# Layer 0 of a two-layer graph network: VectorE multiplies all eight pairs of gathered chunks by their attention weights, ScalarE none

## The chip, the cores and the metric

The program runs on one core of one Trainium2 chip. The core has a matrix engine (TensorE, PE in the profile), three engines for elementwise work (VectorE = DVE, ScalarE = ACT, GpSimd = POOL), a queue for plain transfers (SP) and 16 DMA engines. The metric is the time of one whole execution on the device, in microseconds (us), as the median of several runs. Lower is better.

## What is computed

There are 6250 nodes with 512 features each and 100000 edges. Two layers run one after the other; the change is in the first, a graph attention layer with 8 heads of 64 columns. Cut to what matters:

```python
for h in range(8):
    feat = x @ W[h]
    logit = leaky_relu((feat @ a1)[src] + (feat @ a2)[dst], 0.2)
    m = segment_max(logit, src)
    e = exp(logit - m[src])
    att = e / segment_sum(e, src)[src]
    agg = segment_sum(att[:, None] * feat[dst], src)
    outs.append(relu(agg))
x = x + concatenate(outs, axis=1)
```

The second layer (a graph convolution and a linear attention over the first 256 nodes, with two batch norms) is the same before and after, as is the sorting of the edges that goes ahead of the first.

## The kernel before

**Data.** The edges are sorted by source node and laid out in chunks of 128 slots. Sixteen chunks are a batch, and there are 55 batches. Two chunks of one tile of 128 source nodes are a pair, or "lot"; a batch has eight lots, numbered 0 to 7. For each chunk GpSimd issues one gather (line 503) of 128 rows of 528 floats from `feat_table` in HBM into the ring `ring`, a part of the buffer `big` with room for two batches. A row holds 8 heads of 65 columns (64 features and a one, so that the weights are summed along) and 8 logits of the target node.

**One pass.** The function `pass_batch` of each engine handles two batches at once: it sums up the lots of the batch `this` and prepares the weights of the batch `nxt`. The order on each engine is written out by hand, lot by lot (`a` = 0 to 7). The lot `a` of `this` needs three steps:

- its 2 x 520 columns in the ring are multiplied by their attention weights, in place. On VectorE this is `weigh(b, a)` (line 678), one instruction for both chunks with the weights read from PSUM. It is done for lots 0 to 5 (`OWN` = 6). For lots 6 and 7 it is ScalarE's `weigh_late` (line 553), 16 instructions for a lot, one for each chunk and head, since ScalarE takes one scale for each partition and so one column of weights at a time. ScalarE reads them from `late_weights` in SBUF, into which VectorE copies them once a batch (line 676) ahead of `weigh(b, 0)`;
- TensorE's `lot(b, a)` (line 796): four float32 matmuls against the one-hot matrix of the slots' nodes, into `psA` for even and `psB` for odd lots;
- VectorE's `add_lot(b, a)` (line 688): the sums in PSUM are added to the tile's rows in `acc`. `lot(b, a + 2)` may begin only then, and GpSimd may issue the two gathers of the next batch but one into the same place of the ring as soon as the matmuls of the lot are through (`lot_ps`).

**The weights of the next batch** are made in between, in a chain that goes from engine to engine: ScalarE copies the gathered logits (564), TensorE turns them (765, behind lot 3), ScalarE copies the result (566), VectorE takes running maxima over it (`local_runs`, 616 to 621), TensorE sums the chunks' ends over partitions (769), VectorE carries the maxima over (`carry_runs`, 628 to 640), TensorE spreads them (774), VectorE takes the running maxima again (`find_tops`, 647 to 658), ScalarE makes the exponential (545), and TensorE turns the weights into PSUM (779). Only then can `weigh(nxt, 0)` start. TensorE also turns the one-hot matrix (756) and looks up logits (747) for the batch after, for which VectorE makes the transposed one-hot matrix (600) in two halves.

On VectorE the order from lot 3 on is: `add_lot(this, 3)`, `local_runs`, `carry_runs`, `add_lot(this, 4)`, second half of line 600, `find_tops`, `add_lot(this, 5)`, `add_lot(this, 6)`, line 676, `weigh(nxt, 0)`, `weigh(nxt, 1)`, `add_lot(this, 7)`. On ScalarE the 16 scalings of lot 6 stand at the start of a pass, and those of lot 7 behind the copies of the indices (527).

Of the kernel before, what the change touches and what calls it, by code (L numbers as in the profile page):

```python
# [92 lines left out]
def build(nc, x, src, dst, W0, att_w, norm1_g, norm1_b, norm2_g, norm2_b, W_conv, b_conv, Wq, Wk, Wv, Wo, proj, out):  # L93
    with ExitStack() as ctx:
        def sb(name, shape, dt):
            return ctx.enter_context(nc.sbuf_tensor(name, shape, dt))
# [4 lines left out]
        def sem(name):  # L101
            return ctx.enter_context(nc.semaphore(name))
# [143 lines left out]
        late_weights = sb("late_weights", [P, 4 * H], F32)  # L246
# [101 lines left out]
        late_known = sem("late_known")  # L348
        late_weighted = sem("late_weighted")
# [8 lines left out]
        OWN = LB - 2  # L358
# [166 lines left out]
        def layer0_scalar(act, link, links, clear_rest):  # L525
# [21 lines left out]
            def weigh_late(b, a):  # L547
                act.wait_ge(late_known, b(1, 1))
                for u in (2 * a, 2 * a + 1):
                    for h in range(H):  # L550
                        part = ring[:, b.k, u, h * HO:(h + 1) * HO]
                        at = (u - 2 * OWN) * H + h
                        ins = s.activation(part, part, ACT.Copy, scale=late_weights[:, at:at + 1])  # L553
                    ins.then_inc(late_weighted, 1)

            def feed(b, this=None):

                if this:
                    for a in range(OWN, LB - 1):
                        weigh_late(this, a)  # L560
# [9 lines left out]
                if this:  # L570
                    weigh_late(this, LB - 1)
# [18 lines left out]
            for a in range(OWN, LB):  # L590
                weigh_late(batch(BATCHES - 1), a)

            layer1_scalar(act, link, links, put_indices)

        def layer0_vector(dve, link, links):
# [75 lines left out]
            def weigh(b, a):  # L671
                if a == 0:
                    dve.wait_ge(weights_turned, b(1, 1))
                    dve.wait_ge(scale_done, b(1, 1))
                    wait_count(dve, late_weighted, b(2 * (LB - OWN), 0))
                    v.tensor_copy(late_weights[:, 0:2 * (LB - OWN) * H], weight_ps[b.k][:, 2 * OWN * H:P]).then_inc(late_known, 1)
# [14 lines left out]
            def pass_batch(this, nxt):  # L691
# [4 lines left out]
                for a in range(LB):  # L696
                    if this:
                        if 2 <= a + 2 < OWN:
                            weigh(this, a + 2)
                        if a == 0:  # L700
                            rescale(this, tiles[0])
# [38 lines left out]
        def layer0_tensor(pe, turn_fields):  # L740
# [44 lines left out]
            def lot(b, a):  # L785
# [3 lines left out]
                if a < OWN:  # L789
                    pe.wait_ge(weighted, b(OWN, a + 1))  # L790
                else:
                    pe.wait_ge(late_weighted, b(2 * (LB - OWN), 2 * (a + 1 - OWN)))
# [1729 lines left out]
```

## Time and profile before

| | us |
|---|---|
| median of 3 runs | 3545.59 |
| lowest and highest of them | 3543.25, 3546.13 |
| span of the profiled execution | 3572.6 |

| engine, whole span | busy us | share |
|---|---|---|
| PE matmul | 2678.2 | 75% |
| PE weight load | 1671.6 | 47% |
| DVE | 2439.1 | 68% |
| ACT | 994.4 | 28% |
| POOL | 1863.4 | 52% |

The span is that of one execution under the profiler, 27 us over the median of the runs, which are timed without it; the time around its span is not recorded separately. The batches of layer 0 fill the stretch from 472 to 1904 us. In the rows below a line of the timeline gives the start, the duration, the engine, the line of the code and the tiles, and in brackets how long the engine sat idle before it and what ended that. "Remote" stands where no event in the profile was found that ended the wait, "issue" where the engine waited for nothing that the profile shows.

### The profile page before, as it was taken

What the parts mean: (1) busy time and instruction counts of PE and PEld (TensorE: products, weight loads), DVE (VectorE), ACT (ScalarE), POOL (GpSimd) and SP (SyncE); (2) the same over time, 40 slices, a digit from 0 to 9 for tenths busy, and PEclk for the clock granted to TensorE, in tenths of its full rate; (3) what the DMA queues carried; (4) which work ended last, traced back from release to release, by engine and by line L of the source; (5) the groups of instructions that cost most, each with busy time, mean ns of one, the idle gap of its engine ahead of it and who ended that gap; (6) DMA issues with size and microseconds to landing.
All of it is one profiled execution on the core that took longest, in us unless ns stands there. A gap on an engine that the chain in (4) does not pass through costs nothing. (4 is left out here: it accounts for less than half of the span.)

```text
span 3572.6 us, 49438 instructions
## 1 busy us (share of the span) xinstructions
PE 2678.2 (75%) x11236; PEld 1671.6 (47%) x11237; DVE 2439.1 (68%) x4270; ACT 994.4 (28%) x3078; POOL 1863.4 (52%) x1887
## 2 busy tenths in 40 slices
PE   6887367777787777778777777777777778778991
PEld 4554246665665666566666642322233333233440
DVE  9999956766666666667678745555555556566668
ACT  6733334443444444434443420000000000000220
POOL 0000255555555555555556446666666666663667
PEclk8988678998899898989898888888888889989995
DMA  5110366666666666666655856555555655654226
GB/s 183 46 40 31 103 175 188 189 184 187 175 187 186 183 190 180 187 183 186 184 189 189 265 161 183 171 174 174 173 171 174 175 170 175 177 169 152 68 68 246
DMA packets 243499, 588.70 MB, mean 165 GB/s; under 512 B 57744, under 2 KB 82832, under 8 KB 243400
## 3 DMA queue, kind: packets, MB, share of 16 engines
q0 software_dynamic: 133120, 443.52, 42.8%
q1 hardware_dynamic: 110280, 144.14, 12.3%
q14 instruction: 72, 0.59, 0.1%
q8 instruction: 27, 0.44, 0.1%
HBM read 533.43 MB, written 54.10 MB: 164 GB/s over the span
## 5 line engine op out<-in xcount | busy, mean ns | idle before, releaser
L503 POOL DMA_INDIRECT big<-feat_table,idx x880 | 835.6, 950 | 1031.9 <-ACT idx L527 409.1
L1131 POOL DMA_INDIRECT big<-h_table,idx x784 | 741.6, 946 | 473.5 <-issue 229.3
L796 PE MATMUL psA<-big,onehot 128*128 128x260 f32 x1760 | 481.3, 421 | 92.4 <-DVE big L678 72.9
L796 PE MATMUL psB<-big,onehot 128*128 128x260 f32 x1760 | 496.2, 431 | 28.4 <-DVE acc L688 22.6
L553 ACT ACTIVATE big<-big,late_weights 128x65 f32<-128x65 f32 x1760 | 434.1, 341 | 0.0
L796 PEld LDWEIGHTS psA<-big,onehot 128*128 128x128 f32 x1760 | 352.5, 207 | 171.8 <-issue 91.0
L796 PEld LDWEIGHTS psB<-big,onehot 128*128 128x128 f32 x1760 | 358.9, 214 | 102.2 <-DVE acc L688 34.9
L1854 PE MATMUL psA<-big,onehot 128*128 x556 | 316.9, 694 | 111.2 <-issue 83.9
L1854 PE MATMUL psB<-big,onehot 128*128 x556 | 299.6, 662 | 82.1 <-issue 42.9
L527 ACT CAST idx<-minorB 128x8 int32 (+1 forms) x101 | 20.3, 203 | 1154.6 <-DMA big<-h_table,idx 1154.6
L1566 DVE TENSOR_TENSOR acc<-acc,psA 128x512 f32 x278 | 190.6, 686 | 154.3 <-issue 64.1
L1566 DVE TENSOR_TENSOR acc<-acc,psB 128x512 f32 x278 | 190.6, 685 | 129.6 <-issue 42.1
L1854 PEld LDWEIGHTS psA<-big,onehot 128*128 128x128 f32 x556 | 112.5, 216 | 267.2 <-issue 266.0
L1854 PE MATMUL psCD<-big,onehot 128*128 x276 | 161.3, 669 | 85.8 <-issue 57.6
L1854 PEld LDWEIGHTS psB<-big,onehot 128*128 128x128 f32 x556 | 111.6, 212 | 232.9 <-issue 232.8
L678 DVE TENSOR_TENSOR big<-big,psCD 128x1040 f32<-128x1040 f32 x168 | 203.8, 1227 | 2.1 <-issue 2.0
L688 DVE TENSOR_TENSOR acc<-acc,psB 128x520 f32 x220 | 152.0, 691 | 69.5 <-PE psA L796 34.6
L678 DVE TENSOR_TENSOR big<-big,psE 128x1040 f32<-128x1040 f32 x162 | 196.6, 1227 | 0.0
L2436 PE MATMUL psB<-big 128*128 128x512 f32 x392 | 186.1, 619 | 0.0
L1882 PE MATMUL psA<-big 128*128 128x512 f32 x392 | 180.3, 603 | 0.3 <-ACT big L1297 0.3
L688 DVE TENSOR_TENSOR acc<-acc,psA 128x520 f32 x220 | 152.5, 693 | 37.4 <-issue 6.8
L1854 PE MATMUL psE<-big,onehot 128*128 x276 | 157.5, 655 | 13.0 <-issue 6.9
(442 smaller groups left out, 3805.5 us busy)
## 6 DMA issues: line engine op xcount, KB each, us to landing
nodes_all<-slot_nodes SPq DMA_DIRECT2D x56, 512.0 KB
big<-feat_table,idx POOLq DMA_INDIRECT x880
feat_table<-big SPq DMA_DIRECT2D x49, 264.0 KB, 2.1
x_table<-acc SPq DMA_DIRECT2D x49, 256.0 KB, 3.7
h_table<-big SPq DMA_DIRECT2D x49, 256.0 KB, 3.9
big<-h_table,idx POOLq DMA_INDIRECT x784
big<-h_table SPq DMA_DIRECT2D x49, 256.0 KB, 2.6
big<-x_table SPq DMA_DIRECT2D x49, 256.0 KB, 4.4
```

Of the source, the lines that this page charges most:

```text
L503: g.indirect_dma_start(ring[:, b.k, q * SB + u, :], None, feat_table, bass.IndirectOffsetOnAxis(ap=idx[:, 2 * b.k + q, u:u + 1], axis=0)). ...
L527: s.copy(idx[:, q, :], minor_t[:, :, bass.ds(r, 1)].rearrange("p b a -> p (b a)")).then_inc(signal, 1)
L553: ins = s.activation(part, part, ACT.Copy, scale=late_weights[:, at:at + 1])
L678: v.tensor_tensor(pair, pair, weight_ps[b.k][:, 2 * a * H:(2 * a + 2) * H] .rearrange("p (b h) -> p b h", h=H).unsqueeze(3).broadcast_to([ ...
L688: v.tensor_tensor(d, d, (psA, psB)[a % 2][:, :].rearrange("p (u w) -> p u w", u=2)[:, :, 0:HALF_W], ALU.add).then_inc(lot_added, 1)
L796: ins = pet.matmul(psum[:, 512 * hf:512 * hf + HALF_W], onehot[:, q, u % SB, :], ring[:, b.k, u, HALF_W * hf:HALF_W * (hf + 1)], start=(u ...
L1131: g.indirect_dma_start(big[:, place:place + D], None, h1_table, bass.IndirectOffsetOnAxis(ap=idx[:, r.c % CHUNK_CYCLE, b:b + 1], axis=0)). ...
L1566: v.tensor_tensor(d, d, lot1_sums(r, b), ALU.add).then_inc(lot1_added, 1)
L1854: pet.matmul(lot1_sums(r, b), onehot[:, r.q, b, :], big[:, bass.ds(at[b % 4], D)], start=True, stop=True).then_inc(lot1_ps, 1)
L1882: ins = pet.matmul(psA[:, q * 512:(q + 1) * 512], aggT[:, q, k * P:(k + 1) * P], Wc_s[:, k, :], start=(k == 0), stop=(k == KD - 1))
L2436: pet.matmul(psB[:, q * D:(q + 1) * D], hTbuf[:, q, k * P:(k + 1) * P], W4[:, k, :, :].rearrange("p h o -> p (h o)"), start=(k == 0), stop ...
```

## The change

VectorE runs `weigh` for lots 6 and 7 too, so that each batch has eight of them and `OWN` goes. The 32 scalings of a batch on ScalarE, the copy of 32 columns of weights into `late_weights` and that tile itself, and two semaphores go as well. TensorE waits for `weighted` ahead of each lot.

```diff
@@ ScalarE
-            def weigh_late(b, a):
-                act.wait_ge(late_known, b(1, 1))
-                for u in (2 * a, 2 * a + 1):
-                    for h in range(H):
-                        part = ring[:, b.k, u, h * HO:(h + 1) * HO]
-                        at = (u - 2 * OWN) * H + h
-                        ins = s.activation(part, part, ACT.Copy, scale=late_weights[:, at:at + 1])
-                    ins.then_inc(late_weighted, 1)
-
             def feed(b, this=None):
-                if this:
-                    for a in range(OWN, LB - 1):
-                        weigh_late(this, a)
                 act.wait_ge(rows_arrived[b.k], b.pair(16 * CH, 16 * CH))
...
                     put_indices(minorA, b(2, 4 + q), 2 * b.k + q, idx2)
-                if this:
-                    weigh_late(this, LB - 1)
                 make_weights(b)
@@ VectorE
                     dve.wait_ge(scale_done, b(1, 1))
-                    wait_count(dve, late_weighted, b(2 * (LB - OWN), 0))
-                    v.tensor_copy(late_weights[:, 0:2 * (LB - OWN) * H], weight_ps[b.k][:, 2 * OWN * H:P]).then_inc(late_known, 1)
...
                 for a in range(LB):
                     if this:
-                        if 2 <= a + 2 < OWN:
+                        if a + 2 < LB:
                             weigh(this, a + 2)
@@ TensorE, lot
-                if a < OWN:
-                    pe.wait_ge(weighted, b(OWN, a + 1))
-                else:
-                    pe.wait_ge(late_weighted, b(2 * (LB - OWN), 2 * (a + 1 - OWN)))
+                pe.wait_ge(weighted, b(LB, a + 1))
```

VectorE's queue between `add_lot(this, 3)` (the last 128x520 row at the top) and the end of `local_runs`, in the pass of an odd batch. Before:

```order
L688 TENSOR_TENSOR acc<-acc,psB 128x520
L130 ISA
L130 TENSOR_LOAD tables
L615 REGISTER_ALU
L616 SCALAR_TENSOR_TENSOR alphas<-alphas 128x128 [waits logit_kept]
```

With the change (line 665 is the former 688, 655 the former 678, 595 the former 616):

```order
L665 TENSOR_TENSOR acc<-acc,psB 128x520
L130 ISA
L130 TENSOR_LOAD tables
L655 TENSOR_TENSOR big<-big,psCD 128x2x520
L594 REGISTER_ALU
L595 SCALAR_TENSOR_TENSOR alphas<-alphas 128x128 [waits logit_kept]
```

The multiplication for lot 6 stands ahead of the wait for `logit_kept`. Further down in the same pass, VectorE from the end of `carry_runs` (640) to `find_tops` (647). Before:

```order
L640 TENSOR_TENSOR look_space<-look_space 8x16 [waits carry_step]
L684 REGISTER_ALU
L687 REGISTER_ALU [waits lot_added]
L688 ISA [waits lot_ps]
L688 TENSOR_TENSOR acc<-acc,psA 128x520
L385 REGISTER_ALU
L600 TENSOR_SCALAR big<-nodes_all,iota_col 128x1024 [waits turned_ps]
L647 TENSOR_TENSOR look_space<-psE,chunk_of 128x32 [waits carry_done]
```

With the change (619 is the former 640, 579 the former 600, 626 the former 647):

```order
L619 TENSOR_TENSOR look_space<-look_space 8x16 [waits carry_step]
L661 REGISTER_ALU
L664 REGISTER_ALU [waits lot_added]
L665 ISA [waits lot_ps]
L665 TENSOR_TENSOR acc<-acc,psA 128x520
L655 TENSOR_TENSOR big<-big,psCD 128x2x520
L381 REGISTER_ALU
L579 TENSOR_SCALAR big<-nodes_all,iota_col 128x1024 [waits turned_ps]
L626 TENSOR_TENSOR look_space<-psE,chunk_of 128x32 [waits carry_done]
```

The multiplication for lot 7 stands between `add_lot(this, 4)` and the wait for `turned_ps`.

## Rows read from the trace of the kernel before

**Rows 1.** Page, costliest groups: count, then busy us and mean ns of one.

```profile
L503 POOL DMA_INDIRECT big<-feat_table,idx x880 | 835.6, 950 | 1031.9 <-ACT idx L527 409.1
...
L553 ACT ACTIVATE big<-big,late_weights 128x65 f32<-128x65 f32 x1760 | 434.1, 341 | 0.0
...
L678 DVE TENSOR_TENSOR big<-big,psCD 128x1040 f32<-128x1040 f32 x168 | 203.8, 1227 | 2.1 <-issue 2.0
...
L678 DVE TENSOR_TENSOR big<-big,psE 128x1040 f32<-128x1040 f32 x162 | 196.6, 1227 | 0.0
```

**Rows 2.** Line 676, even batches: min/median/max ns, first and last start.

```profile
L676 DVE COPY late_weights<-psCD x28: 181/190/192, 472.2 to 1887.2; 128x32 f32<-128x32 f32 x28
```

**Rows 3.** Windows, length; busy us (instructions) of PE, PEld, DVE, ACT, POOL; PEclk, DMA, GB/s.

```profile
472.18:1867.29 1395.11, 1084.52 (x5721) 850.32 (x5721) 951.77 (x1908) 597.00 (x2173) 800.61 (x845) 0.90 0.64 185
1867.29:1887.24 19.95, 18.16 (x110) 14.21 (x109) 17.70 (x38) 11.26 (x41) 3.11 (x4) 1.00 0.21 67
```

**Rows 4.** Waits, 460 to 1910 us: total us, times, longest us.

```profile
POOL big L503 <- PE psA L796: 148.7, 87, 13.8
POOL big L503 <- PE psB L796: 128.5, 71, 3.0
...
POOL big L503 <- remote: 109.4, 45, 3.0
...
DVE big L600 <- remote: 97.6, 30, 9.9
...
DVE look_space L630 <- remote: 79.3, 27, 4.6
DVE late_weights L676 <- remote: 73.4, 27, 3.8
...
DVE alphas L616 <- issue: 25.0, 11, 3.8
```

**Rows 5.** Timeline, a batch whose long stop is ahead of line 600.

```profile
1790.17 0.18 DVE L676 COPY late_weights<-psCD 128x32 f32<-128x32 f32 x1
...
1805.67 0.23 PE L769 MATMUL psE<-look_space,head_of 128*8 128x32 f32 x2 [0.98 <-DVE look_space L621]
1805.83 0.62 PE L756 MATMUL psCD<-ident_bf,big 128*128 128x128 bf16 x8
...
1807.57 0.16 DVE L630 TENSOR_TENSOR look_space<-psE,look_space 8x16 f32<-8x16 f32 x1 [1.89 <-remote]
...
1808.35 0.70 DVE L688 TENSOR_TENSOR acc<-acc,psA 128x520 f32 x1
...
1809.14 0.95 POOL L503 DMA_INDIRECT big<-feat_table,idx  x1 [0.30 <-issue]
...
1811.99 0.49 DVE L600 TENSOR_SCALAR big<-nodes_all,iota_col 128x1024 bf16<-128x1024 bf16 x1 [2.94 <-remote]
...
1812.86 0.94 POOL L503 DMA_INDIRECT big<-feat_table,idx  x1 [2.77 <-PE psA L796]
...
1816.31 0.18 DVE L676 COPY late_weights<-psE 128x32 f32<-128x32 f32 x1
```

**Rows 6.** Timeline, a batch whose long stops are ahead of lines 630 and 676.

```profile
1422.04 0.19 DVE L676 COPY late_weights<-psCD 128x32 f32<-128x32 f32 x1 [1.62 <-remote]
...
1439.22 0.16 DVE L630 TENSOR_TENSOR look_space<-psE,look_space 8x16 f32<-8x16 f32 x1 [2.81 <-remote]
...
1443.71 0.33 PE L779 MATMUL psE<-ident_wide,look_space 128*128 128x128 f32 x1
...
1448.84 0.19 DVE L676 COPY late_weights<-psE 128x32 f32<-128x32 f32 x1 [3.78 <-remote]
```

**Rows 7.** Timeline, line 630 in the batch without gathers.

```profile
1880.62 0.16 DVE L630 TENSOR_TENSOR look_space<-psCD,look_space 8x16 f32<-8x16 f32 x1 [0.27 <-PE psCD L769]
```

**Rows 8.** Timeline: the shortest of the batches under gathers, its two ends.

```profile
1027.59 0.19 DVE L676 COPY late_weights<-psE 128x32 f32<-128x32 f32 x1 [1.63 <-remote]
...
1051.84 0.18 DVE L676 COPY late_weights<-psCD 128x32 f32<-128x32 f32 x1
```

More of the change, by code:

```diff
@@ L245, in build @@
         factor = carve("look", 1)
-        late_weights = sb("late_weights", [P, 4 * H], F32)
         factors = carve("look", H)
@@ L347, in build @@
         weighted = sem("weighted")
-        late_known = sem("late_known")
-        late_weighted = sem("late_weighted")
         lot_ps = sem("lot_ps")
@@ L357, in build @@
         RING_CREDIT = 2 * LB
-        OWN = LB - 2
         FREE_CHUNKS = SB * D // ROW_W
@@ L589, in layer0_scalar @@
                     feed(Batch(i, c + 1), Batch(i, c))
-            for a in range(OWN, LB):
-                weigh_late(batch(BATCHES - 1), a)
             layer1_scalar(act, link, links, put_indices)
```

## The prediction

> **What bounds the kernel now.** I read the costliest groups first, then the windows over layer 0, then the waits there, then the timeline of single batches. Only layer 0's batches are touched: line 676 runs once in each of the 55 batches, first at 472.2 and last at 1887.2 us [rows 2], so 54 batches take (1887.2 - 472.2) / 54 = 26.2 us each.
>
> No engine is full there. Up to 1867 us, in 1395 us, VectorE is busy 952, which is 17.8 us of each 26.2 us batch (68%), TensorE 1085, ScalarE 597, GpSimd 801 [rows 3]. So VectorE has some 8 us of idle time in a batch, and the question is whether the added work falls into it. The batch that runs while nothing is gathered any more takes 19.95 us, with VectorE busy 17.70 of them [rows 3]: without gathers the hand-made order runs almost without a stop on VectorE, and the other 6.2 us of a normal batch come with the gathers.
>
> GpSimd issues 16 gathers a batch, each 0.95 us [rows 1] with 0.30 us behind it (the idle time shown in front of one in the middle of a run [rows 5]): 16 x 1.25 = 20.0 us. The rest is stops, in which it waits for a lot to be through so that its place in the ring is free: 148.7 + 128.5 + 109.4 = 387 us in all, 7.2 a batch [rows 4].
>
> The timeline shows that GpSimd's long stop and VectorE's end together. In one batch TensorE ran the transposes of line 756 at 1805.83 for 0.62 us, but VectorE, which waits for them alone ahead of line 600, went on only at 1811.99; GpSimd issued its last allowed gather at 1809.14 and the next at 1812.86 [rows 5]. The lot that it waited for stands right behind the transposes on TensorE. In another batch VectorE stops ahead of 630 until 1439.22 and ahead of 676 until 1448.84, though TensorE had run line 779 at 1443.71 [rows 6]. Without gathers the stop ahead of 630 is 0.27 us [rows 7]. So what TensorE finishes late in a long run of gathers is heard of by the others only when that run has ended. I call this **the hold**. The rows show it, not its cause. It costs VectorE 97.6 us ahead of 600, 79.3 ahead of 630 and 73.4 ahead of 676 [rows 4].
>
> By the Trainium skill (TensorE: Matmul & The Clock Gate, section "The cost: per-tile semaphore tail") increments on completion of matmuls follow each other by some 26 ns, so that a signal of TensorE would be heard at once. This trace does not agree if the records of TensorE are taken as they stand: the gap from 1806.45, where the transposes end, to 1811.99 is 5.5 us. If the page is right here as well, the stops have another cause, and the second rival below is what would follow.
>
> **The change part by part.**
>
> *Two more multiplications on VectorE:* 2 x 1.227 us [rows 1] = 2.45 us a batch, 135 us for all 55. VectorE's busy time in a batch goes from 17.8 to 20.1 us of 26.2.
>
> *The copy of the weights goes:* 0.19 us on VectorE [rows 2], on the path, since weigh(nxt, 0) stands behind it. Part of it overlaps the next instruction, so 0.1 to 0.19; I take 0.15. TensorE also loses one or two register instructions a lot, which I cost at nothing: it is idle in every batch; if they were on the path this would be a gain of some 0.1 us a lot at most.
>
> *ScalarE's scalings go:* 434.1 us of busy time [rows 1], 7.9 a batch. They lie beside other work: those of lot 6 are followed by a wait for the gathered rows, those of lot 7 by one for VectorE's maxima, and no row of the waits has line 553 as the releaser. I take 0. The bounds are 0 and a gain of the same 0.15 us a batch, if one of ScalarE's copies comes earlier now. TensorE's lots 6 and 7 now wait for VectorE, but both products are ready before the add that the lot waits for as well, so the cost is 0; without that cover it would be 1.23 us.
>
> *Place one, weigh 6 ahead of local_runs.* Where VectorE waits there anyway (25.0 us, 11 times, 2.3 each), the 1.23 us are hidden. Elsewhere line 616 and with it TensorE's 769 come 1.23 us later. Behind that stands everything in the chain: 630 to 640, 774, find_tops, add 5, lot 7.
>
> *Place two, weigh 7 ahead of line 600.* It delays line 600 and find_tops by 1.23 us, unless VectorE would have waited there.
>
> Batches come in two kinds. In **27 of them** VectorE stops ahead of 676, 2.7 us on average, and 630 has a long stop as often, 2.9 us on average [rows 4]. The example took 1448.84 - 1422.04 = 26.80 us, with stops of 2.81 and 3.78 us [rows 6]. If the hold ends when the gathers say so, both additions vanish here: 1.23 before the first stop, 1.23 before the second. What stays is the copy: 27 x -0.15 = -4 us.
>
> In **the other 27** of the 54 there is no stop ahead of 676, and the long one is ahead of 600 (30 times, 3.3 us [rows 4]). The example took 1816.31 - 1790.17 = 26.14 us [rows 5]. Here place one matters. TensorE's 769 stood at 1805.67 and its signal came at 1807.57, already late; that of 756, issued 0.16 us behind, came at 1811.99. Moved by 1.23 us, 769 would stand at 1806.90, later than 756 did, so I expect its signal at 1811.9 too. Then VectorE does after the hold what it did in it: line 630 to the end of add 4, 1807.57 to 1809.05 [rows 5], 1.48 us, and weigh 7, 1.23 us, so that line 600 comes 2.7 us later. That is the upper end for this kind: 27 x 2.7 = 73 us. The lower end is that such a batch then becomes one of the first kind, where later stops give most of it back: 26.80 - 26.14 = 0.66 us, 27 x 0.66 = 18 us. No row is nearer to one of these, so I take the middle, 46 us.
>
> Sum: 46 - 4 = **+42 us** (between +14 and +69), +0.8 us a batch. The last batch prepares nothing, and its two added multiplications pair with adds at 1.23 + 0.69 us a lot, about the 1.9 that a lot takes on TensorE: 0 to 2 us, I take 2. So +44. Against the profiled execution: 3572.6 + 44 = 3617 us of span. The runs without the profiler are 27 us shorter (median 3545.6), and I expect the same distance after: **3590 us**, 1.2% slower.
>
> **The rivals.**
>
> *Fully hidden (no change).* If 769 still slips through ahead of the hold in the second kind, both additions fall into stops there too: place one into 630's, place two into 600's. It leaves 54 x -0.15 = -8 to 0 us: 3538 to 3546. For it: VectorE's stops ahead of 616, 630, 600 and 676 sum to 275 us, twice what is added. Against it: 769 would have to move by 1.23 us in a stretch where 0.16 us already made 4.4 us of difference.
>
> *Fully added.* If the stops begin where VectorE arrives and keep their length, instead of ending at a set time, nothing is hidden: 54 x (2.45 - 0.15) = 124 us, 3670 us. For it: the whole chain goes through VectorE, and in the batch without gathers it was idle only 2.25 us [rows 3]. Against it: GpSimd's stop ends together with VectorE's.
>
> *Faster.* The mechanism is the number of GpSimd's stops. Later sums on VectorE shift when lots become free; where two stops of the gathers merge into one, a batch is like the shortest that the trace has, 1051.84 - 1027.59 = 24.25 us [rows 8], 1.95 less than the mean. The price is -1.95 us a batch; against the forecast's 44 us it decides from 23 of the 54 batches. In a third more of them without the cost, 18 x 1.95 = 35: 3510 us. For it: the period is set by gathers and stops, not by VectorE's work. Against it: nothing in the change brings a lot forward; it can only be luck of phase.
>
> *That it doesn't do what it says* can be left out: the order shows eight multiplications a batch on VectorE and none on ScalarE.
>
> **How the numbers follow.** The forecast (partly hidden, 3560 to 3615) has a chance of 0.55, fully added or worse 0.15, fully hidden 0.15, faster by merged stops 0.15. The range leaves out the lower two thirds of the last and what is beyond full addition: 3530 to 3670. A measurement of this kernel can tell 0.2%, 7 us, from no change. Faster by more than that: 0.15 and a little of the hidden case, 0.17; within: 0.13; slower: 0.70.
>
> **What would show it right or wrong in the profile of the changed kernel.** Multiplications on VectorE 440 at 1.23 us, ScalarE's busy time down by 434 us; if one of them lasts longer than 1.23, a term is missing. Period of the batches near 27.0 us; 26.1 would speak for fully hidden, 28.5 for fully added. The stops ahead of 600 should shrink and those ahead of 630 and 676 become more frequent (over 35 of 54 each): place one pushed 769 into the hold. If instead the four stops on VectorE keep their total of 275 us, the additions were not absorbed anywhere. The batch without gathers should take 19.95 + 2.3 = 22.3 us, since little is idle there. The forecast is wrong at its root if GpSimd's stops (7.2 us a batch) shrink while VectorE's work grows.

## The result, and the profile after

| | before | after |
|---|---|---|
| median of 20 runs each, us | 3542.82 | 3551.26 |
| lowest and highest | 3531.82, 3558.64 | 3537.79, 3563.67 |
| ratio, 95% interval | | 1.0025 [1.0015, 1.0034] |
| span of the profiled execution | 3572.6 | 3551.2 |
| mean batch in that execution, us | 26.3 | 26.2 |

The change costs 8 us, a fifth of the 44 forecast. The time is inside the range given and the sign is right, but what happened is the rival "fully hidden", not the forecast. (That the profiled execution after is the shorter one is the scatter of single executions: on one chip a second pair of profiled executions gave 3538.0 before and 3551.7 after.) A batch is measured here from the start of one `weigh(nxt, 0)`, the first multiplication of VectorE for a batch, to the start of the next. There are 54 such stretches; the mean is over the first 53, and the last one, in which almost nothing is gathered, is given by itself further down.

The page of the kernel after, the engines' busy time and the costliest groups; lines 499 and 655 are the former 503 and 678, as in [rows 1]:

```profile
PE 2649.2 (75%) x11236; PEld 1651.3 (46%) x11237; DVE 2559.8 (72%) x4325; ACT 571.9 (16%) x1318; POOL 1863.9 (52%) x1887
...
L499 POOL DMA_INDIRECT big<-feat_table,idx x880 | 836.9, 951 | 1019.5 <-ACT idx L523 407.8
...
L655 DVE TENSOR_TENSOR big<-big,psCD 128x1040 f32<-128x1040 f32 x224 | 273.1, 1230 | 37.5 <-remote 33.8
L655 DVE TENSOR_TENSOR big<-big,psE 128x1040 f32<-128x1040 f32 x216 | 263.3, 1229 | 42.6 <-remote 42.6
```

There are 224 + 216 = 440 multiplications, at 1.23 us as before. ScalarE's busy time is down from 994.4 to 571.9, VectorE's up from 2439.1 to 2559.8. So the work moved as said and at the duration said; the open question is only where 121 us of VectorE's time went.

Windows over layer 0 in the kernel after, columns as in [rows 3]:

```profile
472.00:1904.00 1432.00, 1099.58 (x5916) 865.57 (x5916) 1108.60 (x2030) 194.94 (x486) 808.94 (x852) 0.91 0.63 184
```

DMA share and GB/s are within 0.01 and 1 of [rows 3]. VectorE is now busy 77% of the stretch. Its waits and GpSimd's, 460 to 1910 us, to be held against [rows 4]; line 609 is the former 630, 579 the former 600, 626 the former 647:

```profile
POOL big L499 <- PE psB L770: 175.9, 84, 3.4
...
POOL big L499 <- PE psA L770: 119.2, 107, 12.9
...
POOL big L499 <- remote: 79.9, 34, 2.6
...
DVE big L655 <- remote: 76.4, 34, 2.4
...
DVE look_space L609 <- remote: 40.3, 18, 3.5
...
DVE look_space L626 <- remote: 35.9, 8, 5.4
...
DVE big L579 <- remote: 19.7, 13, 13.2
```

GpSimd's stops are where they were: 375 us in these three rows against 387. VectorE's have shrunk: ahead of line 579 from 97.6 to 19.7, ahead of 609 from 79.3 to 40.3. (Of the 97.6 and the 19.7 one stop each, 9.9 and 13.2 us, lies ahead of the first of these batches; within them it is 87.7 against 6.5.) All idle gaps of VectorE over 0.3 us between the first and the last batch, added up from the timeline, went from 401 to 274 us, by 127. That is about what was added (121). **The added work went into VectorE's stops, and the stops of the gathers, which set the period, stayed.**

The timeline of one batch of the kernel after, columns as in [rows 5], between the two first multiplications:

```profile
1026.93 0.94 POOL L499 DMA_INDIRECT big<-feat_table,idx  x1 [1.10 <-PE psA L770]
...
1035.67 0.95 POOL L499 DMA_INDIRECT big<-feat_table,idx  x1 [0.30 <-issue]
...
1037.10 0.28 PE L746 MATMUL psCD<-look_space,head_of 128*8 128x32 f32 x2 [2.57 <-DVE look_space L600]
1037.31 1.03 PE L733 MATMUL psCD<-ident_bf,big 128*128 128x128 bf16 x8
...
1038.41 0.16 DVE L609 TENSOR_TENSOR look_space<-psCD,look_space 8x16 f32<-8x16 f32 x1 [1.31 <-PE psCD L746]
...
1039.15 0.94 POOL L499 DMA_INDIRECT big<-feat_table,idx  x1 [2.53 <-remote]
...
1039.89 1.23 DVE L655 TENSOR_TENSOR big<-big,psE 128x1040 f32<-128x1040 f32 x1
1041.04 0.55 DVE L579 TENSOR_SCALAR big<-nodes_all,iota_col 128x1024 bf16<-128x1024 bf16 x1
...
1044.16 0.33 PE L756 MATMUL psCD<-ident_wide,look_space 128*128 128x128 f32 x1
...
1047.83 2.39 DVE L655 TENSOR_TENSOR big<-big,psCD 128x1040 f32<-128x1040 f32 x2 [2.34 <-remote]
```

Line 746 is the former 769, 733 the former 756, 756 the former 779. The ends' matmul (746, it sums the chunks' ends) is over at 1037.38 and line 609 goes on at 1038.41, 1.03 us later. Weigh 7 runs at 1039.89, and behind it line 579, which used to stand still for the transposes [rows 5], starts with no wait at all: by then their signal has come. The stop that is left is the one ahead of the next batch's first product, 2.34 us.

### The profile page after: what moved, and what is told of

It reads as the page before. It is cut to its first block and busy times, and to the rows that moved or that the text cites. A ratio compares the mean times of both kernels' runs of the same rounds, so it can differ in the third digit from the quotient of the medians.

```text
span 3551.2 us, 47733 instructions
## 1 busy us (share of the span) xinstructions
PE 2649.2 (75%) x11236; PEld 1651.3 (46%) x11237; DVE 2559.8 (72%) x4325; ACT 571.9 (16%) x1318; POOL 1863.9 (52%) x1887
## 5 line engine op out<-in xcount | busy, mean ns | idle before, releaser
L770 PE MATMUL psA<-big,onehot 128*128 128x260 f32 x1760 | 453.2, 402 | 98.5 <-DVE big L655 80.1
L770 PE MATMUL psB<-big,onehot 128*128 128x260 f32 x1760 | 506.0, 438 | 11.1 <-issue 6.4
L770 PEld LDWEIGHTS psA<-big,onehot 128*128 128x128 f32 x1760 | 331.4, 196 | 174.4 <-DVE big L655 95.0
L770 PEld LDWEIGHTS psB<-big,onehot 128*128 128x128 f32 x1760 | 368.8, 220 | 82.3 <-issue 19.5
L1828 PE MATMUL psA<-big,onehot 128*128 x556 | 306.2, 675 | 101.0 <-issue 63.8
L655 DVE TENSOR_TENSOR big<-big,psCD 128x1040 f32<-128x1040 f32 x224 | 273.1, 1230 | 37.5 <-remote 33.8
L655 DVE TENSOR_TENSOR big<-big,psE 128x1040 f32<-128x1040 f32 x216 | 263.3, 1229 | 42.6 <-remote 42.6
L1828 PEld LDWEIGHTS psA<-big,onehot 128*128 128x128 f32 x556 | 110.9, 213 | 254.1 <-issue 253.8
L1828 PEld LDWEIGHTS psB<-big,onehot 128*128 128x128 f32 x556 | 109.6, 208 | 237.3 <-issue 236.7
L1540 DVE TENSOR_TENSOR acc<-acc,psCD 128x512 f32 x138 | 94.6, 685 | 72.2 <-issue 29.6
```

The source lines that it names most:

```text
L655: v.tensor_tensor(pair, pair, weight_ps[b.k][:, 2 * a * H:(2 * a + 2) * H] .rearrange("p (b h) -> p b h", h=H).unsqueeze(3).broadcast_to([ ...
L770: ins = pet.matmul(psum[:, 512 * hf:512 * hf + HALF_W], onehot[:, q, u % SB, :], ring[:, b.k, u, HALF_W * hf:HALF_W * (hf + 1)], start=(u ...
L1540: v.tensor_tensor(d, d, lot1_sums(r, b), ALU.add).then_inc(lot1_added, 1)
L1828: pet.matmul(lot1_sums(r, b), onehot[:, r.q, b, :], big[:, bass.ds(at[b % 4], D)], start=True, stop=True).then_inc(lot1_ps, 1)
```

## The experiments

Each of the five groups of runs had a chip of its own, and these are of **two kinds**; all runs of a group are of the same kind. On kind A the kernel before takes 3538 to 3544 us, as in the result above; on kind B it takes 3032 to 3038. Ratios are to the kernel before on the same chip. The runs do not say what makes a chip one or the other. The recorded expectations speak of three theories: A, the stops that come with the gathers hide VectorE's added work; B, ScalarE's relief gives as much back as the added work costs, gathers or not; C, added after the first group, on a chip without late signals GpSimd's 16 issues set the batch.

| kernel | kind | median us | ratio [95%] | batch us |
|---|---|---|---|---|
| ng_before | B | 2978.57 | 0.9812 [0.9785, 0.9838] | 19.53 |
| ng_after | B | 3064.20 | 1.0083 [1.0052, 1.0114] | 21.14 |
| minus2 | B | 3031.95 | 0.9991 [0.9980, 1.0002] | 20.57 |
| plus2 | B | 3182.68 | 1.0487 [1.0457, 1.0517] | 23.30 |
| before_again | A | 3549.31 | 1.0011 [0.9995, 1.0027] | 26.08 |
| after_again | A | 3553.78 | 1.0015 [0.9992, 1.0037] | 26.09 |
| plus1 | A | 3552.37 | 1.0014 [0.9993, 1.0034] | 26.12 |
| sprows_after | A | 3278.47 | 0.9242 [0.9195, 0.9290] | 21.35 |
| after_third | B | 3068.63 | 1.0127 [1.0100, 1.0153] | 21.19 |
| plus2_again | B | 3183.16 | 1.0499 [1.0479, 1.0518] | 23.29 |
| plus4 | B | 3294.39 | 1.0866 [1.0847, 1.0885] | 25.29 |
| paced_after | B | 3062.54 | 1.0104 [1.0085, 1.0123] | 21.05 |
| eight_after | A | 3397.91 | 0.9609 [0.9579, 0.9639] | 23.33 |
| spaced_after | A | 3828.10 | 1.0825 [1.0796, 1.0854] | 31.24 |
| plus2_c | A | 3572.98 | 1.0117 [1.0086, 1.0149] | 26.54 |
| plus4_c | A | 3626.54 | 1.0257 [1.0225, 1.0290] | 27.34 |
| pace4_before | B | 3196.05 | 1.0522 [1.0505, 1.0540] | 23.46 |
| pace2_before | B | 3353.63 | 1.1045 [1.1026, 1.1063] | 26.46 |

The theory from here on: on the chip of the result the gathers and the late signals set the end of VectorE's stops, so that work put ahead of them is free until the stops are used up. The rival: VectorE's chain sets the period, and something else hid the work.

### First group (kind B): no gathers, and VectorE's work per batch changed by two products

Both kernels without gathers leave out those of the batches 2 to 54, so that old rows are summed; in ScalarE's code the wait for them goes to a constant:

```diff
-            with pool.Fori(1, BATCHES // 2) as i:
-                for c in range(2):
-                    gather_batch(Batch(i, c))
-            gather_batch(batch(BATCHES - 1))
...
-                act.wait_ge(rows_arrived[b.k], b.pair(16 * CH, 16 * CH))
+                act.wait_ge(rows_arrived[b.k], 16 * CH)
```

> Kernel before, but GpSimd gathers rows only for batches 0 and 1; the later batches weigh and sum what lies in the ring already, so their neighbours' features are left out. Theory A (the stops that come with the gathers hide VectorE's added work): every batch runs as the last one of the kernel before did, 19.95 us instead of 26.2, so about 54 x 6.25 = 337 us less than 3543, near 3205 us. Theory B (the added work costs nothing because the freed ScalarE gives as much back elsewhere, gathers or not): the same for this kernel.

> The changed kernel with gathers for batches 0 and 1 only, as the other one without gathers. Theory A: with the gathers' stops gone the added 2.3 us a batch are bare, so 124 us over the kernel before without gathers, near 3330 us (up to 54 x 4 = 219 more if its last batch of 24.0 us is the measure). Theory B: within 20 us of the kernel before without gathers.

Windows 500 to 1450 us, columns as in [rows 3], of ng_before and then of ng_after:

```profile
500.00:1450.00 950.00, 885.08 (x5268) 692.43 (x5267) 860.92 (x1759) 542.89 (x1999) 0.00 (x0) 1.00 0.09 29
```

```profile
500.00:1450.00 950.00, 833.88 (x4857) 653.22 (x4856) 889.98 (x1664) 157.27 (x405) 0.00 (x0) 0.98 0.08 26
```

Without gathers VectorE is busy 91% of the time before and 94% after, and a batch grows by 21.14 - 19.53 = 1.61 us. So the added products do cost when nothing else bounds, though 1.6 and not the 2.3 that I took for the batch without gathers: before, VectorE still had idle time, 45 us in gaps over 0.3 us, of which 17 are left after.

The kernel minus2 is the kernel after without the products of lots 6 and 7 (nobody multiplies them):

```diff
-                        if a + 2 < LB:
+                        if a + 2 < LB - 2:
...
-                pe.wait_ge(weighted, b(LB, a + 1))
+                pe.wait_ge(weighted, b(LB - 2, min(a + 1, LB - 2)))
```

> The changed kernel, but lots 6 and 7 are not multiplied by their weights by any engine, which part of layer 0 is left out. Theory A: VectorE's 2.45 us a batch were hidden, so nothing comes back: 3535 to 3551 us. Theory B: the work is on the path and ScalarE's relief stays, so 124 us less: 3427 us.

The kernel plus2 (and plus1, plus4) is the kernel after with two (one, four) small multiplications ahead of each of the products of lots 6 and 7, into a tile that nobody needs then; four of them measured 2.1 us a batch, and plus1's two 0.9:

```diff
+                if a >= LB - 2:
+                    for n in range(2):
+                        wait_count(dve, spared, b(4, (a - LB + 2) * 2 + n))
+                        v.tensor_tensor(maxd[...390 columns...], iota_row[...], weight_ps[b.k][...],
+                                        ALU.mult).then_inc(spared, 1)
```

> The changed kernel with four more VectorE products of 390 columns a batch, two ahead of each of the multiplications of lots 6 and 7, written to a tile that nobody reads; some 0.66 us each with the wait, 2.6 us a batch, 143 us in all. Theory A: VectorE still has 276 us of stops in layer 0, 5.1 us a batch, but some of these are shorter than what is put ahead of them, so a part shows: 20 to 80 us over the changed kernel, 3570 to 3630 us. Theory B: all of it shows, 3690 us.

Window of minus2, same columns:

```profile
500.00:1450.00 950.00, 858.78 (x4998) 667.93 (x4996) 818.30 (x1618) 164.43 (x414) 703.48 (x739) 0.99 0.80 237
```

The kernel minus2 takes as long as the kernel before. On kind B, then, ScalarE's 32 scalings do not bound the kernel before, since a kernel without them and without the products in their place is no faster; GpSimd does, busy 703 of 950 us, which with 0.30 us behind each of the 739 gathers is 925. Its 16 x 1.25 = 20.0 us are all but 0.57 of the batch. The kernel after, at 21.2 us, is above that floor and bound by VectorE, and so plus2 costs in full: 3182.7 - 3068.6 (after_third, below) = 114 us for the 54 x 2.1 = 113 added.

### Second group (kind A): the two kernels again, one product's worth more, and plain transfers

> The kernel before, unchanged, to have its trace from the chip that this call gets. The runs without gathers were on a chip where it takes 3032 us instead of 3543. If the chip is like that one: theory C (no hold there, the batch is paced by GpSimd's 16 issues of 1.25 us) expects batches of 20.3 to 20.8 us and hardly any stop of GpSimd; if the hold is there too, batches of 26 us or more stops. Ratio to itself 1.00.

> The changed kernel, unchanged. Theory C on a chip without the hold: VectorE's chain is barely shorter than GpSimd's 20.3 us there, so the added work shows in part: the batch of 21.1 us of the changed kernel without gathers, against 20.6: 54 x 0.5 to 0.9 = 27 to 49 us, ratio 1.009 to 1.016. Theory A in its old form (always hidden): ratio 1.00. On a chip with the hold both expect 1.0025 again.

> The changed kernel with two more VectorE products of 390 columns a batch, one ahead of each multiplication of lots 6 and 7, 1.3 us a batch, written to a tile that nobody reads. Without the hold, theory C: VectorE is the longest already, all of it shows, 54 x 1.3 = 70 us over the changed kernel. With the hold: under 20 us over it, since VectorE has 5.1 us of stops a batch.

For sprows_after SP fetches rows of the table in plain transfers of the same bytes; GpSimd gathers nothing behind batch 0. Other rows are summed than the reference's:

```diff
+            def plain_rows(b, lots):
+                for a in lots:
+                    sp.wait_ge(lot_ps, b(LB, a + 1))
+                    for u in (2 * a, 2 * a + 1):
+                        sp.dma_start(ring[:, b.k, u, :], feat_table[u * P:(u + 1) * P, :]).then_inc(rows_plain[b.k], 16)
```

> The changed kernel with the gathers of batches 1 to 54 replaced by as many plain transfers of the same size from the SP queue (always the rows of the first 16 tiles, so the choice of rows by edge is left out). If GpSimd's indirect gathers with 1.25 us of issue each pace the batch: batches of 21.1 us as without gathers. If the bytes do it (4.3 MB a batch), the same batches as with gathers: 26 us on a chip with the hold, 20.6 to 21.3 on one without.

The three kernels from before_again to plus1 cannot be told apart, at 26.08, 26.09 and 26.12 us a batch. The kernel plus1 has 0.9 us more on VectorE in each than the kernel after, and its median is within 2 us of that kernel's (added in full it would be 51). With plain transfers a batch falls to 21.35 us, 4.7 less than with gathers. Its timeline, the ends' matmul and the line that waits for it, and its window:

```profile
1006.57 0.23 PE L756 MATMUL psCD<-look_space,head_of 128*8 128x32 f32 x2 [1.97 <-DVE look_space L610]
1006.83 0.16 DVE L619 TENSOR_TENSOR look_space<-psCD,look_space 8x16 f32<-8x16 f32 x1 [0.27 <-PE psCD L756]
```

```profile
1000.00:1300.00 300.00, 264.62 (x1521) 207.05 (x1521) 279.04 (x522) 50.36 (x126) 0.00 (x0) 0.97 0.73 229
```

The matmul ends at 1006.80 and is heard at 1006.83. The DMA engines move more than before (229 GB/s against 185) and still no signal is late. So it is neither the bytes nor the load of the DMA engines; it goes with the gathers that GpSimd issues.

### Third group (kind B): the kernel after again, more work, and increments between gathers

> The changed kernel, unchanged, for the trace and the ratio on this call's chip. With the hold (kernel before at 3543 us): ratio 1.00 to 1.003, batches of 26.1 to 26.3 us. Without it (kernel before at 3032 us): theory C says batches of 21.1 to 21.4 us against 20.5, ratio 1.009 to 1.016.

> The changed kernel with four more products of 390 columns a batch on VectorE, 2.6 us a batch. With the hold: its stops on VectorE are 5.1 us a batch, of which the half-sized addition used up 0.8 without any loss of time; theory A says a batch of 26.3 to 27.0 us, 0 to 38 us over the changed kernel. Without the hold: 150 us over the kernel before, as measured once.

> The changed kernel with eight such products a batch, 5.2 us. VectorE's own work is then 25.4 us a batch, near the 26.2 us of the batch. With the hold, theory A: the stops cannot hide all of it, 27.5 to 29 us a batch, 70 to 150 us over the changed kernel. If stops keep a fixed length instead of ending at a set time, all 5.2 us show, 280 us. Without the hold: 290 us over the kernel before.

```diff
+                            if not under_sort:
+                                for _ in range(5):
+                                    pool.sem_inc(hold, 1)
```

> The changed kernel with five semaphore increments ahead of each gather on GpSimd, so that gathers are issued some 1.5 us apart and no longer 1.25. If the hold comes from gathers issued faster than they are carried out (a backlog), it goes: batches of 24 to 25 us on a chip with it, 60 to 120 us less. If it comes from each gather whatever the distance, the batch gets longer by 16 x 0.25 = 4 us, 200 us more. Without the hold: GpSimd's issue becomes the bound, 24 us a batch, 180 us over the kernel before.

The same place in after_third, which has its gathers at 1.25 us like all others:

```profile
1019.96 0.23 PE L746 MATMUL psE<-look_space,head_of 128*8 128x32 f32 x2 [1.97 <-DVE look_space L600]
1020.23 0.16 DVE L609 TENSOR_TENSOR look_space<-psE,look_space 8x16 f32<-8x16 f32 x1 [0.27 <-PE psE L746]
```

0.04 us from end to start, and so in all of its batches: on kind B there is no hold. Against the kernel after, plus2 costs 114 us and plus4 226, for 113 and 54 x 4.1 = 221 us of added work. There VectorE's chain is the bound and nothing is hidden. The change itself costs 36 us there, a third of the 121 added, since the first part of it fills VectorE's idle time beside GpSimd's 20.0 us.

I had meant paced_after to spread the gathers on a chip with the hold. It shows nothing: it ran on one without, and the increments did not spread them. GpSimd's rows:

```profile
1000.71 1.02 POOL L502 DMA_INDIRECT big<-feat_table,idx  x1 [0.30 <-issue]
1002.03 0.97 POOL L502 DMA_INDIRECT big<-feat_table,idx  x1 [0.30 <-issue]
```

Its batch is 21.05 us, where 24 was expected of spread gathers on such a chip. On plus4 the expectation was 290 us over the kernel before; measured were 262.

### Fourth group (kind A): half the gathers, gathers further apart, and more work

```diff
+                            if not under_sort and q == 1:
+                                continue
```

leaves out the gathers of chunks 8 to 15 of each batch from batch 2 on (ScalarE then waits for half the rows), so that half the rows summed are old, and for spaced_after a small fill on GpSimd, with a wait for it, ahead of each gather:

```diff
+                                g.memset(maxd[...64 columns...], 0.0).then_inc(paced, 1)
+                                pool.wait_ge(paced, b(2 * SB, q * SB + u + 1 - 4 * SB))
+                                pool.sem_inc(hold, 1)
```

> The changed kernel with gathers for the first 8 of 16 chunks of each batch from batch 2 on; the other 8 keep old rows, so their neighbours are left out. With late signals (kernel before at 3543 us): if they need a long run of gathers, runs of at most 8 gathers leave time for them, batches near the 21.2 us that the chain needs by itself, some 270 us less than the changed kernel. If every gather delays signals, batches of 23 to 25 us, 70 to 170 us less. Without late signals (3032 us): 21.0 to 21.2 us a batch, 0 to 10 us less than the changed kernel.

> The changed kernel with a fill of 64 columns on GpSimd and a wait for it ahead of each gather, so that gathers stand some 1.5 us apart and no longer 1.25. With late signals: if they come from a backlog of gathers (265 KB each 1.25 us is some 216 GB/s), it goes, and a batch takes 16 x 1.5 = 24 to 25 us, 60 to 120 us less than the changed kernel. If each gather delays them whatever the distance, the batch gets longer by 16 x 0.25 = 4 us, 200 us more. Without late signals: GpSimd's 24 us are the bound, 3220 us.

> The changed kernel with 2.1 us more work on VectorE in a batch (four products of 390 columns). On the chip without late signals a batch took 23.3 us with it, so as long as that is under the 26.3 us of the late signals, theory A (the stops end at a time that the gathers set) expects 0 to 38 us over the changed kernel. If only stops of a fixed length hide work, all of it shows: 114 us over.

> The changed kernel with 4.1 us more on VectorE in a batch. On the chip without late signals a batch took 25.3 us with it. Theory A: still below 26.3, but few stops are left to hide it: 27 to 28 us a batch, 40 to 100 us over the changed kernel. Fixed stops: 225 us over.

In eight_after all eight gathers of a batch come in one run. Its first and its last, and the ends' matmul behind them:

```profile
1009.88 0.94 POOL L501 DMA_INDIRECT big<-feat_table,idx  x1 [12.63 <-PE psA L772]
...
1018.62 1.01 POOL L501 DMA_INDIRECT big<-feat_table,idx  x1 [0.30 <-issue]
...
1019.47 0.23 PE L748 MATMUL psCD<-look_space,head_of 128*8 128x32 f32 x2 [2.00 <-issue]
...
1021.30 0.16 DVE L611 TENSOR_TENSOR look_space<-psCD,look_space 8x16 f32<-8x16 f32 x1 [1.84 <-remote]
```

The last gather is issued by 1019.63, the matmul ends at 1019.70 and is heard at 1021.30, 11.4 us behind the start of the run. In the batch of the kernel after above it is the same: a run of eight from 1026.93, line 609 at 1038.41, 11.5 us later. In [rows 5] it is 11.6 us. Some signals are heard inside a run, as in [rows 5] that of 769; what is still held then is let go at a time that depends on the length of the run. In the traces of before, before_again, after, after_again and plus1 the first stop of VectorE or ScalarE that ends behind a run ends 5.7 to 6.0 us after the run's start where it has four gathers, 8.6 to 8.7 with six, 11.4 to 11.6 with eight and 12.8 to 13.0 with nine (medians of each trace). That is 1.43 to 1.5 us a gather, against the 1.25 us at which GpSimd issues them, and so 1.0 us behind the end of the last gather's row after four and 1.8 after eight. So the end of the hold is set by the gathers. That is the point on which all hung: VectorE can be late or early, it goes on at the same time.

It looks like a queue that takes 1.43 us for each gather and gets one every 1.25; what it is, no run shows. It is not the arrival of the rows: the last packet of a gather lands 3.4 us after its issue in the median in the kernel after, and 3.5 in after_third on kind B. Nor are all signals late: in the kernel after, TensorE starts its matmul 746 within 0.06 us of the end of the VectorE instruction that it waits for, in every batch.

By its expectation eight_after, 149 us below the kernel after, spoke for a delay by each gather whatever the distance. The next kernel rules that out; it is rather that a run of eight is long enough to hold the ends' matmul for 2.6 us, in 50 of 53 batches.

In spaced_after the gathers are 1.93 us apart where I had expected 1.5:

```profile
1001.27 0.95 POOL L504 DMA_INDIRECT big<-feat_table,idx  x1 [0.81 <-POOL maxd L501]
1002.22 0.17 POOL L501 MEMSET maxd<- 128x64 f32 x1
1003.20 0.95 POOL L504 DMA_INDIRECT big<-feat_table,idx  x1 [0.81 <-POOL maxd L501]
```

The signals of TensorE that I followed there (those of 765, 769, 756 and 779 before) are all heard within 0.05 us, on a chip of kind A, with all gathers running. But 16 x 1.93 = 31 us of GpSimd a batch then bound the kernel, and it is 8% slower. It shows what the hold needs (gathers closer behind each other than 1.93 us), not a way to gain. A distance just over 1.43 us would make 16 x 1.43 = 23 us a batch, under the 26.1; that is an estimate from the rows above, and no run of kind A has it.

The two with more work show where the cover ends. In plus4_c, GpSimd and VectorE around the first product of the next batch:

```profile
1017.20 0.95 POOL L500 DMA_INDIRECT big<-feat_table,idx  x1 [0.31 <-issue]
1019.10 2.39 DVE L662 TENSOR_TENSOR big<-big,psCD 128x1040 f32<-128x1040 f32 x2 [2.00 <-remote]
1019.94 0.94 POOL L500 DMA_INDIRECT big<-feat_table,idx  x1 [1.79 <-PE psB L777]
```

The stop ahead of the first product stays, some 1.7 us in nearly every batch, and the others are used up. VectorE's idle gaps over 0.3 us sum to 401 (before), 274 (after), 201 (plus2_c), 119 (plus4_c). Against it the last batch, in which almost nothing is gathered and which so shows how long the chain takes by itself:

| kernel, kind A | last batch, us | mean batch, us |
|---|---|---|
| before, before_again | 20.0, 19.5 | 26.3, 26.1 |
| after, after_again | 21.6, 22.2 | 26.2, 26.1 |
| plus1 | 21.7 | 26.1 |
| plus2_c | 23.1 | 26.5 |
| plus4_c | 25.3 | 27.3 |

Up to 22 us of chain the mean batch does not move; at 23 it starts to. In plus4_c it is 2.1 us above the chain, most of which is the stop ahead of the first product that stays. On kind B, where there is no such stop, the same kernel (plus4) takes 25.3 us a batch. On the medians, with the kernel after at 1.0025 x 3538.4 = 3547 on this chip: plus2_c costs 26 us of the 113 added, plus4_c 79 of the 221.

### Fifth group (meant for kind A, ran on kind B): a short gap now and then in the gathers

The same fill as above in the kernel before, ahead of every fourth or every second gather:

```diff
+                        if not under_sort and a % 2 == 0:
+                            pool.sem_inc(hold, 1)
+                            g.memset(maxd[...64 columns...], 0.0).then_inc(paced, 1)
+                            pool.wait_ge(paced, b(LB // 2, (q * LOTS + a) // 2 + 1 - 2 * LB // 2))
```

> The kernel before with the fill and its wait (0.68 us) on GpSimd ahead of every fourth gather of a batch. With late signals: if one gap in four gathers lets the signals through, a batch is bound by GpSimd's 16 x 1.25 + 4 x 0.68 = 22.7 us, some 190 us less than the kernel before; if not, gaps only add to the stops, 26 to 28 us a batch, 0 to 80 us more. Without late signals: 22.7 us instead of 20.5, 120 us more.

> The kernel before with the same gap ahead of every second gather. With late signals: if this lets them through, 16 x 1.25 + 8 x 0.68 = 25.4 us a batch, 40 us less than the kernel before; if not, 28 to 30 us a batch. Without late signals: 25.4 us, 270 us more.

GpSimd in pace4_before:

```profile
1004.49 0.95 POOL L508 DMA_INDIRECT big<-feat_table,idx  x1 [0.30 <-issue]
1005.43 0.17 POOL L501 MEMSET maxd<- 128x64 f32 x1
1006.50 0.95 POOL L508 DMA_INDIRECT big<-feat_table,idx  x1 [0.89 <-PE psB L801]
```

A gap adds 2.01 - 1.25 = 0.76 us, four of them 3.0 and eight 6.1 us a batch; measured were (3196.05 - 3037.61) / 54 = 2.9 and 5.9. So on kind B GpSimd's issuing is the bound of the kernel before, nearly to the full. Whether such gaps would break the hold on kind A and pay there, which was the question, is not answered. No kernel that computes the whole reference was faster than the kernel before.

## Why the prediction was right or wrong

**The two products' duration, ScalarE, the copy.** Right: 440 at 1.23 us; ScalarE's busy time fell by 422 us and bought nothing, as said. On kind B minus2, which has neither, equals the kernel before. The copy's 0.15 us a batch, 8 us in all, cannot be told apart here.

**The first kind of batch: both additions vanish in the stops.** Right, and for the reason given: the hold ends when the gathers say so (the ends by length of run under the fourth group, and plus1 at no cost that can be seen).

**The second kind of batch: the step that failed.** I wrote that line 769, moved by 1.23 us, "would stand at 1806.90, later than 756 did, so I expect its signal at 1811.9 too", and priced that at 46 us. But the transposes stand behind 769 on TensorE and move with it. A batch of the kernel after that is as [rows 5], with 769 (now 746) 1.1 us later in a run of eight gathers; the first and the last of the run, and what stands between:

```profile
871.42 0.94 POOL L499 DMA_INDIRECT big<-feat_table,idx  x1 [1.15 <-PE psB L770]
...
877.79 0.23 PE L746 MATMUL psCD<-look_space,head_of 128*8 128x32 f32 x2 [1.48 <-DVE look_space L600]
877.95 0.62 PE L733 MATMUL psCD<-ident_bf,big 128*128 128x128 bf16 x8
...
879.94 0.16 DVE L609 TENSOR_TENSOR look_space<-psCD,look_space 8x16 f32<-8x16 f32 x1 [2.15 <-remote]
...
880.16 0.95 POOL L499 DMA_INDIRECT big<-feat_table,idx  x1 [0.30 <-issue]
...
881.42 1.23 DVE L655 TENSOR_TENSOR big<-big,psE 128x1040 f32<-128x1040 f32 x1
...
882.87 0.49 DVE L579 TENSOR_SCALAR big<-nodes_all,iota_col 128x1024 bf16<-128x1024 bf16 x1 [0.23 <-remote]
```

The matmul ends 6.6 us into the run, later than the transposes did in [rows 5] (6.1), and is heard at 8.5; the transposes are heard at 11.45 (11.6 in [rows 5]), and weigh 7 stands in what was the stop ahead of them. Of the 53 batches 15 have it at 6.6 us, and it is heard there at 7.1 to 9.9, in none at 11.5. So the 46 us of this kind of batch were in truth nothing that can be measured. In the kernel after the ends' matmul is still heard 1.03 us after its end in the median and 3.3 at most (before 1.62 and 4.35), while the transposes, where anyone waits for them, are heard 4.3 us late (before 5.5). (The median for the ends' matmul differs between executions of one kernel, 0.04 us in before_again; that for the transposes hardly.) I had taken a clock reading, 1805.67 late and 1805.83 very late, for a boundary in time. The rows only showed that the second of two neighbouring signals comes much later than the first, and that still holds for the moved pair in the 12 batches where line 579 waits at all. Why it is so stays open. With 769 through, weigh 7 fell into the old stop ahead of line 600, which went from 87.7 to 6.5 us in these batches (from 97.8 to 19.3 between before_again and after_again). This is the condition under which the rival "fully hidden" was to hold, and I had given it 0.15. What I held against it was that same misreading of the 0.16 us.

Taking the middle between 18 and 73 us was a second weakness: both ends assumed that 769 gets stuck, so the bounds did not contain the case in which it does not. The lower bound should have been nothing.

**The last batch.** I took 22.3 us; measured were 21.6 in the profiled execution and 22.2 in the one of after_again. The two profiled executions before have 20.0 and 19.5. So 1.6 to 2.7 us of the 8 may be here, as I had put it (2 us); the mean batch of after_again is 0.01 us over that of before_again, under 1 us in all. Where the rest of the 8 us comes from is below what single executions tell apart.

**The distance to the profiler.** I took the 27 us between the profiled execution and the median for a property of the profiler that would come again. It did not come again: the span after is 3551.2 against a median of 3551.26. The forecast of 3590 did not rest on it, only that of 3617.

**The signs I gave.** Mean batch 27.0 us: it is 26.1 to 26.2, what I had put down for "fully hidden". Stops ahead of 600 shrink: right. Those ahead of 630 and 676 in over 35 of 54 batches each: ahead of the first product 34, ahead of 630 18 marked "remote" and 40.3 us in place of 79.3: wrong, since it was the sign of a 769 that gets stuck. VectorE's four stops keep their 275 us if nothing is absorbed: they shrank (all its gaps by 127 us), so all was absorbed. GpSimd's stops did not shrink: right.

**The rivals.** *Fully added*: ruled out on kind A, and its mechanism (the stops keep their length) with it. On kind B the added work beyond what the change brings is paid in full, but because VectorE is the bound there. *Faster by merged stops*: beyond the 0.30 us behind each gather GpSimd has 178 stops of over 0.5 us after and 180 before, 327 and 339 us; they did not merge. *The Trainium skill's 26 ns* (TensorE: Matmul & The Clock Gate, section "The cost: per-tile semaphore tail"): the page's figure is what one more increment adds on TensorE, and that a signal would be heard at once was my own conclusion from it; no run here measures the spacing of increments. Where there is no hold the traces agree with the conclusion, 0.03 to 0.05 us from the end of a matmul to the waiting instruction, in all kernels on kind B, in sprows_after and in spaced_after. In the gathers' runs on kind A they do not, by up to 5 us and more. So the hold is real and not an error of the records, for the same lines of the same program show 0.04 us elsewhere.

## What to carry to other kernels

Idle time of an engine is cover for added work only if something else sets the moment at which it ends; ask of each stop who ends it, and test that by adding work in steps, for the time stays flat until the cover is used up and then rises (on kind A by 26 us for the first 113 added to the kernel after and by 53 for the next 108; on kind B, without cover, by all of it). When a wait is priced after a shift, shift all that stands around it on the same queue too, and let the lower bound be the case that nothing gets stuck. A verdict holds for the bound of the chip that it ran on: the same edit is 0.25% slower on one kind of chip, where stops that others end hide it, and 1.3% on the other.

## What the runs showed of the hardware

- On chips of kind A, while GpSimd issues gathers of 128 rows at 1.25 us each, signals of TensorE to VectorE, ScalarE and GpSimd are heard late: the transposes that VectorE waits for (ahead of line 600 before, 579 after) 5.5 us in the median before and 4.3 after, for the logits that ScalarE copies 2.0 us in the median and 5.7 at most in the kernel after, for a lot that GpSimd waits for up to 7 us. What is still held is heard 1.0 (after four gathers) to 1.9 us (after eight) behind the last gather of the run, 1.43 to 1.5 us for each gather after its start. Where no run of gathers is on, with the gathers 1.93 us apart, or with plain transfers at 229 GB/s in their place, it is 0.03 to 0.05 us on VectorE and ScalarE. On kind B it is that with gathers at 1.25 us too (GpSimd goes on 0.81 us behind a lot there). What in the chip delays them, and what sets the kinds apart, is open.
- In layer 0 this is 26.2 against 21.2 us a batch for the same kernel. From the first to the last batch it took 1408 us on kind A and 1145 on kind B, so 263 of the 483 us between the two kinds are here. GpSimd pays it: it waits for signals of TensorE that come only when it has stopped issuing, 327 us of stops over 0.5 us in the kernel after on kind A and 49 on kind B. The rest of the difference lies outside layer 0's batches and was not looked into.
- Products on VectorE kept their 1.23 us under gathers, plain transfers and neither: only signals were late, not data.
- The granted clock of TensorE does not tell the kinds apart: 0.91 in layer 0 of the kernel after and 0.97 in sprows_after, both on kind A; 1.00 in ng_before, 0.98 in after_third and 0.89 in plus4, all on kind B.
- Five semaphore increments ahead of each gather on GpSimd left the spacing at 1.25 to 1.3 us; a fill of 64 columns with a wait for it adds 0.7 to 0.8.
